# A graph layer with experts: the expert stage in row-major tiles of 128, and two smaller moves

## The reference

```python
x = x + gnn(xn, src, dst) + mix(xn)       # two graph convolutions; linear attention, 16 heads
x = x + ffn(layernorm(x))
# ffn: 8 experts, the two best for each row
logits = flat @ Wr.T
weights, ids = top_k(logits, 2); weights = softmax(weights)
h = einsum('nc,efc->nef', flat, W1)        # W1: 8 x 512 x 1024
act = h[..., :256] * silu(h[..., 256:])
out = sum over the two experts of weights * (act @ W2[e].T)   # W2: 8 x 1024 x 256
```

## Time and profile before

| what | value |
|---|---|
| median of 3 runs | 1486.6 us (1482.56 to 1492.09) |
| the profiled execution's own time | 1488.26 us |
| its span, first to last instruction | 1486.6 us |
| PE busy | 1409.2 us, 95% |
| mean granted clock | 0.979 of full speed |
| first matmul of the expert stage | 1213.28 us |
| last matmul of it ends | 1473.32 us |

### The profile page before, as it was taken

How to read it: one execution, slowest core, us unless ns; L and a number is a source line. 1 busy time by engine, 2 the same in 40 slices (tenths; PEclk the granted TensorE clock), 3 DMA queues, 4 the chain that set the end, 5 groups by cost and what they waited for, 6 DMA issues and landing times.

```text
span 1486.6 us, 19993 instructions
## 1 busy us (share of the span) xinstructions
PE 1409.2 (95%) x7691; PEld 1303.4 (88%) x7691; DVE 866.1 (58%) x1567; ACT 536.0 (36%) x621; POOL 184.8 (12%) x182
## 2 busy tenths in 40 slices
PE   6999999999999999988999999999999859999996
PEld 5888899999999999888999999999788648888885
DVE  6564678778778778625666324354667744433330
ACT  4233254354354355232122233322112235444441
POOL 0012210100110111000000000000001442223321
PEclk9999999999999999998999999999999869999998
DMA  9755433243233336675543042221565587887864
GB/s 316 241 151 122 78 52 80 45 83 74 51 80 72 56 80 211 229 168 152 134 121 87 15 129 81 84 80 46 159 177 153 158 226 198 211 217 180 195 154 83
DMA packets 97217, 194.34 MB, mean 131 GB/s; under 512 B 31745, under 2 KB 62456, under 8 KB 95403
## 3 DMA queue, kind: packets, MB, share of 16 engines
q1 hardware_dynamic: 76353, 145.83, 33.2%
q0 software_dynamic: 20768, 47.22, 17.4%
HBM read 129.78 MB, written 73.13 MB: 136 GB/s over the span
## 4 chain that ended last, share of the span: by engine, by line
PE 71%; DMA 14%; DVE 7%; ACT 3%; issue 3%; SPq 1%; POOLq 0%; POOL 0%; ACTq 0%; DVEq 0%
PE slot L1853 23%; PE slot L1937 12%; DMA adj_d<-stage 7%; PE slot L2081 7%; PE slot L2049 6%; PE slot L2011 5%; PE slot L1809 3%; PE kvb L2081 3%; PE kvb L1975 3%; PE slot L1795 2%; DMA adj_d<-eye_dram 2%; PE slot L2064 2%; DMA mix_d<-mix_half 1%; PE slot L1960 1%; DMA dx<-x_dram 1%
## 5 line engine op out<-in xcount | busy, mean ns | idle before, releaser
L1853 PE MATMUL slot<-big_hi,slab_h 128*128 128x418 f32 x768 | 195.1, 362 | 14.8 <-DVE mixn L1484 7.2
L1853 PE MATMUL slot<-big_lo,slab_h 128*128 128x418 f32 x768 | 189.8, 355 | 0.0
L1853 PE MATMUL slot<-big_hi,slab_l 128*128 128x418 f32 x768 | 188.4, 353 | 0.0
L1853 PEld LDWEIGHTS slot<-big_hi,slab_h 128*128 128x128 f32 x768 | 140.5, 190 | 19.8 <-DVE mixn L1484 7.6
L1853 PEld LDWEIGHTS slot<-big_hi,slab_l 128*128 128x128 f32 x768 | 145.5, 190 | 2.3
L1853 PEld LDWEIGHTS slot<-big_lo,slab_h 128*128 128x128 f32 x768 | 145.5, 190 | 2.3
L846 POOL DMA_DIRECT2D adj_d<-stage x80 | 66.7, 833 | 484.6 <-ACT stage L924 392.4
L1937 PE MATMUL slot<-adj,xs_h 125*128 125x418 f32 x480 | 118.1, 354 | 0.5 <-DVE ztmp L1176 0.5
L1937 PE MATMUL slot<-adj,xs_l 125*128 125x418 f32 x480 | 117.4, 353 | 0.0
L1180 DVE TENSOR_SCALAR oh_src<-lane,src_lo 125x125 bf16<-125x125 f16 x320 | 84.0, 263 | 26.5 <-PE kvb L1680 19.1
L871 POOL DMA_INDIRECT list_d<-rec,spots x20 | 27.9, 1397 | 528.3 <-issue 511.0
(11 more groups left out here) (319 smaller groups left out, 2943.7 us busy)
## 6 DMA issues: line engine op xcount, KB each, us to landing
slab_raw<-slabs_dram SPq DMA_DIRECT2D x40, 512.0 KB, 4.3
ws_raw<-w_dram SPq DMA_DIRECT2D x36, 512.0 KB, 7.9
adj_d<-stage POOLq DMA_DIRECT2D x81, 117.2 KB, 3.1
w_raw<-w_dram SPq DMA_DIRECT2D x9, 1024.0 KB, 7.8
adj_d<-eye_dram POOLq DMA_DIRECT2D x1, 6250.0 KB, 24.4
raw<-adj_d SPq DMA_DIRECT2D x3, 1828.8 KB
dx<-x_dram SPq DMA_DIRECT2D x10, 448.0 KB
xn_d<-dx SPq DMA_DIRECT2D x10, 448.0 KB
```

Source lines behind the costliest of these rows:

```text
L1853: mm = ten.matmul(ps[:, 512 * q:512 * q + CW], w[a][:, kt, :], big[b][:, kt, CW * q:CW * q + CW], start=(kt == 0 and c == 0), stop=(kt == ...
```

## The change

The expert stage has no round loop. Each expert has three tiles of 128 list rows (384 rows), 24 tiles in all, written out. A tile is row-major: the transposed rows are stationary (128 columns) and the weights move, 512 columns at once, gate and value side by side, 24 matmuls into one bank (`GV`). Silu and product are of 128 rows by 256 (`SM`); two transposes turn the result (`TR`), which is split, and 12 matmuls of 512 columns follow (`OUT`). PE does the transposes of tile n+1 after k-step 1 of tile n, the `TR` of tile n-1 after k-step 3, and the `OUT` of tile n-1 behind the whole of tile n. W1 comes in four slabs of two k-steps, with room for two experts.

List rows beyond 384 of an expert are items of 128 rows. After the 24 tiles a loop runs over the items, at least once; the expert's weights are loaded by a register. The loop is skewed: its body ends tile 23 (or the item before), then makes gate and value of this item; the end of the last item stands behind the loop. DVE finds the next item with a chain of small operations. By the lists above there is one item, the ninth to last rows of expert 3.

The pieces of a list load are 8 bytes (they were 32). `KK` 0 and 1 of pairs 1 to 7 move into `Q`, after k-steps 5 and 6. `deg_part[0]` gets a place of its own, `deg_part[1]` the one over `mix_half[0]`, and the wait for the stores moves from part 0 to part 1.

```diff
     for p in range(PAIRS):
         more = p + 1 < PAIRS
-        o += [("KK", p, 0), ("KK", p, 1), ("KK", p, 2)]
+        o += [] if p else [("KK", p, 0), ("KK", p, 1)]
+        o.append(("KK", p, 2))
         if p:
             last = WITHIN[("Q", p)][1]
             o += [("EP", last), ("E", last)]
...
+        o += [("EO", q0), ("AT", p, 1), ("EO", q1), ("E", q0), ("RC", p), ("KK", p + 1, 0),
+              ("KK", p + 1, 1), ("Q", p + 1)]
     for f in range(KD):
         if f == KD - 1:
...
 INNER |= {k for p in range(PAIRS - 1) for k in (("S", p), ("QP", p, 0, 1), ("AT", p, 0), ("QP", p, 1, 0), ("QP", p, 1, 1))}
 OTHER = INNER | {("QP", p, 0, 0) for p in range(PAIRS - 1)}
...
-            before[k] = last.get(turn) if k[2] == 0 else before[("KK", k[1], 0)] if k[2] < 3 else ("KK", k[1], k[2] - 3)
-            last[turn] = k
+            place[k] = 1 - turn if k in INNER else turn
+            before[k] = (last.get(place[k]) if k[2] == 0 else before[("KK", k[1], 0)] if k[2] < 3
+                         else ("KK", k[1], k[2] - 3))
+            last[place[k]] = k
...
 SLOT, BEFORE = places_of()
 
 
-RT_ = 105
-NRT = 4
-CAP = NRT * RT_
-ROUNDS = -(-N // CAP)
-LIST = ROUNDS * CAP
-HALVES = FF // 128
-WS = 2 * HALVES
+RT_ = 128
+PER = 3
+CAP = PER * RT_
+LT = -(-N // RT_) + PER
+LIST = LT * RT_
+DUMMY = EXP * LT
+TILES = EXP * PER
+MAX_ITEMS = EXP * (LT - PER)
+GAP = 1000.0
+SLABS_PER = 4
...
+def expert_steps():
+
+    o = [("WP", m) for m in range(SLABS_PER)] + [("W2P", 0), ("XE", 0)]
+    for n in range(TILES):
+        e, i = divmod(n, PER)
+        if e + 1 < EXP:
+            o += ([("W2P", e + 1)] if i == PER - 1 else
+                  [("WP", SLABS_PER * (e + 1) + 2 * i), ("WP", SLABS_PER * (e + 1) + 2 * i + 1)])
+        if n >= 2:
+            o.append(("OUT", n - 2))
+        if n + 1 < TILES:
+            o.append(("XE", n + 1))
+        if n >= 1:
+            o.append(("TR", n - 1))
+        o.append(("GV", n))
+        if n < TILES - 1:
+            o.append(("SM", n))
+    return o + [("OUT", TILES - 2)]
+
+
+STEPS = expert_steps()
+R_ACT = numbered({"WP", "W2P", "XE", "SM", "TR", "OUT"}, STEPS)
+R_DVE = numbered({"WP", "W2P", "XE", "SM", "TR"}, STEPS)
+ORDERED_PE = []
+for _n in range(TILES):
+    ORDERED_PE += [("XE", _n + 1)] if _n + 1 < TILES else []
+    ORDERED_PE += ([("TR", _n - 1)] if _n else []) + [("GV", _n)] + ([("OUT", _n - 1)] if _n else [])
+R_FULL = numbered({"XE", "TR", "GV", "OUT"}, [("XE", 0)] + [k for k in ORDERED_PE if k != ("GV", TILES - 1)])
+SCATTERED = [len(range(s, TILES - 1, NY)) for s in range(NY)]
...
         mixt = at("mixt", R + 75776, [128, NP])
-        deg_part = [at(f"deg_part{h}", R + (66912, 68608, 80896)[h], [T, CW], F32R) for h in range(3)]
...
+        xe_p = [[at(f"xe_{'hl'[q]}{s}", 8192 * s + 4096 * q, [128, KD, RT_], F32R) for q in range(2)] for s in range(2)]
+        ws_p = [[at(f"ws_{'hl'[q]}{s}", 16384 + 8192 * s + 4096 * q, [128, 2, 512], F32R)
+                 for q in range(2)] for s in range(2 * SLABS_PER)]
...
 
-        list_d = nc.dram_tensor("list_d", [EXP * LIST, 2], F32, kind="Internal").ap()
```

SP and POOL (the loop bodies of the old rounds are gone):

```diff
+            list_tiles = list_d.rearrange("(t q) w -> t q w", q=RT_)
+            for e in range(EXP):
+                sp.dma_start(lists[:, PER * e:PER * e + PER, :],
+                             list_tiles[LT * e:LT * e + PER].rearrange("i q w -> q i w")).then_inc(list_landed[min(e, 2)], 16)
+            for k in STEPS:
+                if k[0] == "WP" and k[1] + SLABS_PER < SLABS_PER * EXP:
+                    sp.wait_ge(expert_dve, R_DVE[k])
+                    load_ws(k[1] + SLABS_PER)
+                elif k[0] == "W2P" and k[1] + 1 < EXP:
+                    sp.wait_ge(expert_dve, R_DVE[k])
+                    load_w2(k[1] + 1)
...
+            sp.wait_ge(items_ready, 1)
+            items = sp.value_load(items_n[0:1, 0:1], min_val=1, max_val=MAX_ITEMS)
+            sp.wait_ge(item_made, 1)
+            tile = sp.value_load(item_x[0:1, 1:2], min_val=0, max_val=DUMMY)
+            sp.dma_start(lists[:, TILES, :], list_tiles[bass.ds(tile, 1), :, :].rearrange("i q w -> (i q) w")
+                         ).then_inc(item_list_landed, 16)
+            with sp.Fori(0, items) as r:
+                sp.wait_ge(item_made, r + 1)
...
+                owner = sp.value_load(item_x[0:1, 0:1], min_val=0, max_val=EXP - 1)
+                previous = sp.value_load(item_x[0:1, 2:3], min_val=0, max_val=DUMMY)
+                sp.sem_inc(item_read, 1)
+                for m in range(SLABS_PER):
+                    sp.wait_ge(raw_split, r * SLABS_PER + m + 1)
+                    sp.sem_inc(sp_passed, 1)
+                    sp.dma_start(ws_raw[m][:, :, :].rearrange("p a c -> p (a c)"),
+                                 w1[bass.ds(owner * SLABS_PER + m, 1), :, :].rearrange("e p c -> (e p) c")
+                                 ).then_inc(ws_landed[m], 16)
+                sp.wait_ge(w2_split, r + 1)
...
+            for n in range(TILES - 1):
+                if n + NXG - 1 < TILES:
+                    gather(n + NXG - 1)
+                if n and n % PER == 0:
+                    for q in range(NY):
+                        pool.wait_ge(added[q], 16 * len(range(q, n, NY)))
+                pool.wait_ge(expert_act, R_ACT[("OUT", n)])
+                pool.sem_inc(pool_passed, 1)
```

ACT, then DVE:

```diff
+                elif kind == "SM":
+                    full(("GV", n))
+                    if n:
+                        act.wait_ge(expert_dve, R_DVE[("SM", n - 1)])
...
+            def silu_tail(turn, tr_full):
+
+                act.wait_ge(tail_gv, turn)
+                act.wait_ge(expert_dve, R_DVE[("SM", TILES - 2)])
+                act.activation(sil[:, :], gv[1][:, 0:FF], ACT.Silu).then_inc(tail_act, 1)
+                act.wait_ge(tail_full, tr_full)
+                copy(a_p[1][0][:, :, :].rearrange("p f c -> p (f c)"), turned[1]).then_inc(tail_act, 1)
+
+            def out_tail(out_full, listed_, scattered):
+
+                act.wait_ge(tail_full, out_full)
+                act.wait_ge(last_list_landed, listed_)
+                act.wait_ge(added[NY - 1], scattered)
+                copy(y[NY - 1][:, :], wide[1][:RT_, :], scale=lists[:, TILES + 1, 1:2]).then_inc(tail_y, 1)
+
+            act.wait_ge(items_ready, 1)
+            items = act.value_load(items_n[0:1, 0:1], min_val=1, max_val=MAX_ITEMS)
+            with act.Fori(0, items) as r:
+                silu_tail(r + 1, r * 3 + 2)
+                copy(xe_p[0][0][:, :, :], blocks(wide[0], KD, RT_, 128)).then_inc(tail_act, 1)
+                for m in range(SLABS_PER):
+                    if m == 2:
+                        out_tail(r * 3 + 3, r * 16 + 16, r * 16 + 16 * SCATTERED[NY - 1])
+                    act.wait_ge(ws_landed[m], r * 16 + 16 * (EXP + 1))
+                    copy(ws_p[m][0][:, :, :], ws_raw[m][:, :, :]).then_inc(tail_act, 1)
+                act.wait_ge(w2_landed, r * 16 + 16 * (EXP + 1))
...
+                    if h == 1:
                         dve.wait_ge(mix_stored[2], 2 * LAND)
...
+            def next_item(r):
+
+                item_link(dve.tensor_reduce(first, left, AX.X, ALU.min), r)
+                item_link(ts(first, first, DUMMY - GAP, ALU.min), r)
+                item_link(ts(owner_w, item_c[:, 2 * MAX_ITEMS:2 * MAX_ITEMS + 7], first, ALU.is_le), r)
+                item_link(dve.tensor_reduce(owner_n, owner_w, AX.X, ALU.add), r)
+                item_link(dve.tensor_copy(item_x[:, 0:1], owner_n), r)
+                item_link(ts(item_x[:, 1:2], first, GAP, ALU.add), r)
+                item_link(dve.scalar_tensor_tensor(out=left, in0=left, scalar=first, in1=left, op0=ALU.is_gt,
+                                                   op1=ALU.mult), r)
...
+            with dve.Fori(0, items) as r:
+                act_tail(r)
+                dve.wait_ge(tail_act, r * 8 + 3)
+                tt(xe_p[0][1][:, :, :], blocks(wide[0], KD, RT_, 128), xe_p[0][0][:, :, :].bitcast(F32), ALU.subtract
+                   ).then_inc(tail_xe, 1)
+                for m in range(SLABS_PER):
+                    dve.wait_ge(tail_act, r * 8 + m + 4)
+                    tt(ws_p[m][1][:, :, :], ws_raw[m][:, :, :], ws_p[m][0][:, :, :].bitcast(F32), ALU.subtract
+                       ).then_inc(raw_split, 1)
+                dve.wait_ge(tail_act, r * 8 + 8)
+                tt(w2_p[1][1][:, :, :], w2_raw[:, :, :], w2_p[1][0][:, :, :].bitcast(F32), ALU.subtract
+                   ).then_inc(w2_split, 1)
+                dve.wait_ge(item_read, r + 1)
+                item_link(ts(item_x[:, 2:3], first, GAP, ALU.add), r)
+                next_item(r)
+                dve.sem_inc(item_made, 1)
+            act_tail(items)
 
 
```

PE:

```diff
+            def key_features(k):
+
+                p, i = k[1:]
+                if i == 0:
+                    ten.wait_ge(dve_done, DVED[("K", p)])
+                for h in range(2):
+                    for c, part in enumerate((proj_h, proj_l[h])):
```

(97 more changed lines are left out.)

486 lines of the change are left out of this document (236 added, 250 removed).

## The result

The changed kernel took 1468.7 us (median of 4 runs, 1466.1 to 1471.1) against 1489.3 us for the kernel before on the same chip: ratio 0.986, 95% interval 0.983 to 0.990. Its profiled execution took 1471.0 us with a span of 1469.3, where the one before had 1488.26 and 1486.6. On a second chip it took 1467.2 us, ratio 0.985 [0.983, 0.987]. The forecast was 1464 us, range 1453 to 1481, mostly "faster by over 1%".

The account below looks back on a forecast made before the run. PE, with work for 95% of the span, was taken as the bound. Expert stage 12.9, degrees 9.5 and key features 2.0 sum to 24.4 us off 1488.26: 1463.9, predicted 1464 us, range 1453 to 1481.

Parts of the forecast that it names:

- The tiles: Expert stage: an expert's three row-major tiles take 28.7 us of PE instead of 32.5, 9.6 a tile, with no inner waits.
- the rival of 0.7 us a tile: Expert stage: each row-major tile waits 0.7 us, 17 us in all, giving 1481 us; chance 0.13.
- the pace of the 512-column matmul with 128 stationary columns: Expert stage tiles: taken as 0.235 us a matmul, between 0.234 and 0.28.
- The start: Expert stage: one tile's gather is enough, first transposes at 1204.3, first `GV` at 1208.8, list pieces costing 0.7 us.
- the splits ... hidden by the gather: Start of the expert stage: DVE's splits of four slabs and W2 end at 1202, hidden by the gather.
- Tail and end: After `GV` 23: 28.3 us to the last matmul for one item (bounds 24 and 36), then 1.2 and 10.6 to the end.
- the 0.7 that was taken: Start of the expert stage: cost of list loads in 8-byte pieces, taken as 0.7 us, at most 3 us later.
- Degrees: Degree phase: PE's 7.23 us wait and the slow restart go, 10.0 us, of which 9.5 is taken; bounds 0 and 10.
- That may cost PE 0.5: Degree phase: the next mix copy waits for the previous store, its load moved earlier into a full DMA queue; 0.5 us.
- PE waits at slab `O` 4 or 5: Degree phase: a sign by which the prediction falls; it expected no idle PE after slab `O` 3.
- Key features: Pairs of heads: DVE does `kk_l` 0 ahead of PE, saving 0.28 us in seven pairs, 2.0 us; bounds 0 and 3.4.
- The first `GV`: Sign in the new trace: first `GV` near 1197, which is 1208.8 less 11.5.

Follow-up runs that it names:

- experiment 8: Changed kernel with the output product of tiles 12 to 22 made with 105 stationary columns instead of 128: 1469.9 us, ratio 0.987.
- experiment 5: Changed kernel with expert 1's weight loads held on SP until PE has turned the first gathered tile: 1467.2 us, ratio 0.985.
- experiment 10: Changed kernel with weight loads held until the first gather lands, mix store ahead of raw adjacency loads, and next-item chain between slab splits: 1458.9 us, ratio 0.979.
- experiment 11: Changed kernel with only expert 1's weight loads held on SP until the first gather has landed: 1464.7 us, ratio 0.982.
- Experiment 7: Changed kernel with DVE's small operations for the next item put between the splits of slabs 1 and 2: 1463.4 us, ratio 0.982.
- experiment 1: Kernel before with the degree edit alone (`deg_part` places, wait moved to part 1): 1482.1 us, ratio 0.995.
- experiment 6: Changed kernel with the store of the third mix slab issued ahead of the last two raw adjacency loads: 1463.9 us, ratio 0.984.
- experiment 2: Kernel before with the key feature edit alone: 1489.5 us, ratio 0.999 [0.998, 1.000].
- experiment 3: Changed kernel with the degree and key feature edits undone, leaving the expert stage alone: 1475.2 us, ratio 0.991.
- experiment 4: Changed kernel made to run two passes of its item loop, the second on an empty list: 1497.3 us in one run.
- experiment 12: Changed kernel with two passes of the item loop and DVE's next-item chain between the splits of slabs 1 and 2: 1482.7 us in one run.

## Why the prediction was right

- **The tiles.** The mechanism held: no wait inside a tile, and the rival of 0.7 us a tile is out (PE's waits of the stage are those of its start and tail). The size was 9.31 us for the forecast 9.6. The mis-sized term is the pace of the 512-column matmul with 128 stationary columns: 0.227 us for `OUT` and 0.229 for `GV`, outside the bounds 0.234 to 0.28. From the start of `GV` 0 to the end of `GV` 23 it was 219.2 us, not 224.8: 5.6 better. Why the pace is better than the old 0.235 is open; experiment 8 gives the width 0.003 of it.
- **The start** was the step that failed: "the splits ... hidden by the gather" counted the loads at nothing. `GV` 0 starts 21.2 us after the scatter that follows `spots`; the forecast had 16.8. 4.4 us: the gather (8.6 against 4.6 us from issue to PE's transposes) is 4.0 of them, the scatter of the pairs 0.9 (3.8 us to landing, 2.6 before; why was not looked for), and smaller terms give 0.5 back. The step moved was DVE's slab splits, and what SP issues behind them was not followed past POOL's gather. Experiments 5, 10 and 11 showed it (4.4 to 5.6 us with the loads held, 6.3 to 9.5 without), and also that only 2.4 us of it come back by holding the loads.
- **Tail and end.** 28.3 us forecast, 28.3 measured: the product behind DVE's chain, the last matmuls at the low clock. Experiment 7 confirms the chain's place on the path. The end was 11.4 us after the last matmul, forecast 11.8; in that sum the 1.85 for the issue stands in no row (the issue in the earlier trace rows is 1.52), but the value taken was a middle one. So the stage gave 14.5 us for 12.9: -4.4, +5.6 and +0.4. That it came out so close is partly luck, since the two larger errors nearly cancel.
- **The Trainium skill** (DMA: Bandwidth & Descriptors, Anatomy of one DMA — SWDGE (gpsimd) path) gives 2.0 us plus bytes over 436 GB/s for one DMA, an estimate of 3.2 us for a gather of 0.5 MB. This case's gather took 4.4 to 5.6 us with the loads held and 8.4 beside them; the measurement decides. It was never quite by itself, since five further gathers are issued behind it, so no run here tests the fit for a transfer alone. The same page says that below 512 bytes a transfer reads, modifies and writes (Specifications). The smaller pieces cost this change 0.3 us in its own trace (a list load of 1.97 us for 1.66), and 0.4 to 1.1 us in ten others, for the 0.7 that was taken.
- **Degrees.** 9.5 forecast, 6.2 in the profiled execution, 7.0 in experiment 1. PE's 7.23 us and the slow restart went, part 1 waits for nothing, as forecast. The term "That may cost PE 0.5" was mis-sized: it was 2.05 us and a slow restart of 1.8. The cause stood in the prediction, the copy that waits for the store and "its load ahead of it"; experiment 6 showed that this load, issued 1.35 us ahead of the store, is what makes the copy late. The prediction named "PE waits at slab `O` 4 or 5" as a sign that it falls, and PE did wait at `O` 5: for this part the sign came true, and the sum held since the part is small.
- **Key features.** 2.0 forecast, 0.25 to 0.31 us a pair seen (1.7 to 2.2 in seven pairs), 1.6 by the ratio of experiment 2 with an interval that reaches nothing. PE's 3.4 us of waits for `kk_l`, which gave the upper bound, are another product's and are there unchanged after; the wait that went is the weight load's 0.28 of the earlier trace rows.
- **The first `GV`** was expected "near 1197" and began at 1210.4. Of these 13 us the late first phase is 4.9, the start 4.4, the degrees 3.3 and the key features 0.6.
- **The first phase.** The profiled executions reach its end at different times, whatever the edit. Its last piece in the chain, before and after the change:

```profile
176.97 3.09 DMA adj_d<-stage
```

```profile
181.88 3.10 DMA adj_d<-stage
```

Between these lie 4.9 us. The same row starts at 180.88 in the changed kernel run again, and at 178.63, 180.19 and 183.35 in experiments 3, 1 and 2, of which the first has all of the expert part and the last none. Experiments 4, 7 and 12 edit only the item chain, far behind this row, and have it at 178.08, 182.33 and 177.99, where the changed kernel has 181.88. Traces with the same lines up to here thus differ by over 4 us, so a stage is to be measured from its own first event.

## What to carry to other kernels

When a step moves earlier, follow what it frees on every queue: here a split done sooner let SP fetch weights beside the one small gather for which all engines waited, and a raw load stood ahead of the one store that was needed next. Of two transfers on a queue, the one that somebody waits for goes first; and a bookkeeping chain that asks for the next list belongs ahead of the work that hides its transfers, which was worth 2 us in the last pass and 8 in each further one.

## What the runs showed that was not expected

- A matmul of 512 columns is not slower with a full stationary tile: 0.227 us at 128 columns, 0.230 at 105 in the same trace.
- The first gather of 128 rows of 4 KB lands in 4.4, 4.5 and 5.6 us with the weight loads held, and in 8.4 in the changed kernel's trace, where 2 MB of slabs are asked for 1.2 us behind it. Seven other executions in that order had 6.3 to 9.5 us.
- The DMA engines moved 413 GB/s in the mean of 1203 to 1215 us, 380 to 452 in single slices, while weights and rows came in from DRAM. The Trainium skill (DMA: Bandwidth & Descriptors, Where 436 GB/s comes from) gives 435 for the ports, with which this mean agrees, and about 358 as what binds transfers between HBM and SBUF, above which it lies.
- With the same waits of 1.1 us ahead of them, the last 12 matmuls took 4.59 and 4.48 us in experiments 7 and 12 (mean granted clock 0.64 and 0.65, so mostly the low one), and 3.02 in experiment 10 (1.00). At slab `O` 5 a wait of 1.77 us was followed by 7.00 us for 27 matmuls, one of 1.88 us by 5.45 (granted clock 0.76 and 1.00). What decides between these was not settled.
